# Attention and state-space layer on one core: first sample's remainders on VectorE, first row of maxima in halves, late inputs moved, the chain into the scan reordered

## The chip, the cores and the metric

The kernel runs on one core of one Trainium2 chip. What counts is its time on the device in microseconds (us). Time before: 542.61 us, median of 3 runs (541.83 to 543.48).

## What is computed

Eight samples of 256 tokens and 256 channels pass two layers, each with a residual. The reference, cut:

```python
# layer 1: modulated attention, 16 heads of 16 channels
x = x * s1; x = (x - mean) * rsqrt(var + 1e-5)
q, k, v = (x @ q_w.T) * q_dc, (x @ k_w.T) * k_dc, (x @ v_w.T) * v_dc * s2
out = softmax(q k^T / 4) v
x = x0 + (out @ w_w.T) * w_dc + (v @ u_w.T) * u_dc
# layer 2: a gated scan over the tokens, 512 channels, 16 states
xr, gate = split(x @ W_in.T); xc = silu(causal_conv4(xr + t_emb) + b_conv)
xn = layer_norm(xc) * ln_g + ln_b
Bm, Cm, dt = split(xn @ W_xproj.T)
Ad = 1 - 0.01 * tanh(dt @ W_dt.T + b_dt) * tanh(A_log)
Bd = Bm * minimum(norm(xn), 1)
def step(h, (ad, bd, xt, ct)):           # 256 steps
    h = clip(h * ad + bd * xt, -10, 10)
    return h, ct . h
return x + ((ys + D * xn) * silu(gate)) @ W_out.T
```

## The kernel before

Each engine has an instruction stream written out by hand, and semaphores order the streams against each other. An engine never takes a later instruction first: whatever stands behind a wait in its stream waits too. SP (and a little ScalarE) issue the DMAs, and SP too is one stream.

**Start.** VectorE multiplies the token tiles by the style (`modulated_statistics`, L1541), takes statistics (L1509, L1512), and makes the roots (`rsqrt`, L1518 to L1526); `demodulate` and a second `rsqrt` make the coefficients `dc`. TensorE transposes and projects (`channels_of`, L1023). q and k of a sample are split in three bf16 parts: ScalarE takes them from PSUM and casts (`take_qk`, L658, L662; `second_cast`, L667), GpSimd takes the two remainders of each (L501, L505, for all samples). The parts are stored to `qk_d` (`store_stack`, L295) and loaded again as a stack of rows per head (`load_stack`, L323), sample 0's in two halves, stacks 0 and 1 before, then x transposed, the in-weights, the norm rows and the out-weights (L364, L367), then stack 2.

**Attention.** For each sample TensorE makes every head's scores twice: once for the maxima (`max_scores`, L1049, reduced by VectorE, L1643), and once for the exponentials (`scores`, L1064; ScalarE, L737), for which the maxima of all heads stand as one more row of the stack. They get there by two transposes (`turn_maxima`, L1089), a copy to `mT` (L720) and a DMA (`take_maxima`, L722). While scores of sample b are made, the maxima of b+1 are. The stream for the first sample:

```python
            max_scores(0, 0, 8)
            pe.wait_ge(s["const_pool"], 1)
            pe.wait_ge(s["wgain"], 1)
            weight_sums()
            max_scores(0, 8, 12)
            pe.wait_ge(s["k_in"], 2)
            transpose_xn(2, 2)
            max_scores(0, 12, 14)
            pe.wait_ge(s["xnT_ready"], 3)
            channels_of(0, 2, "q_done")
            max_scores(0, 14, NH)
```

**Passage.** After the convolution the tiles are normalised on VectorE (`finish`: L1718, L1726). A tile `j` is split into three bf16 parts, `xpart`: the first by ScalarE (`leave_parts`, L851), the remainder by TensorE in PSUM (`first_left`, L1349), the second by ScalarE (`second_part`, L866), then `second_left` (L1356) and the third by VectorE (`last_part`, L1802). B is scaled by the norms (`square`, L859) and split (`split`, L1793 to L1797), stored and loaded across partitions (`store_b`, L273; `load_b`, L281), as are the tiles (`store_parts`, L388; `load_x`, L399). The gates are eight projections (`project_gate`, L1257) that end with `take_gate` (L820).

**Scan.** A step is a product on TensorE (`u_steps`, L1427) and one saturating operation on VectorE (L1834) in a ring of eight tiles `zst`, four of which lie in the in-weights `win`; every four steps TensorE reads the ring out (`y_steps`, L1438). The steps come in tiles of 16, with loads of x and B two tiles ahead on SP.

## Time and profile before

| | us |
|---|---|
| median of 3 runs | 542.61 |
| profiled execution | 539.56 |
| its span, first to last instruction | 537.8 |
| busy in it: TensorE, VectorE, ScalarE, GpSimd | 475.2, 432.0, 256.8, 177.5 |

The profiled execution is one run; its time holds the span and 1.8 us around it. A row of the timeline gives the start, the duration from first to last of its instructions, engine, line, operation and, in brackets, how long the engine sat idle before it and what released it. "q" behind an engine's name is its sequencer, which issues DMAs.

### The profile page before, as it was taken

The numbers are of one execution on the slowest core, as the hardware profiler recorded it, in microseconds if no ns is written. First come the engines' busy times: TensorE is split into PE (matmuls) and PEld (weight loads), VectorE is DVE, ScalarE is ACT, GpSimd is POOL, SyncE is SP. The second block draws the span as 40 slices with busy tenths as digits, with TensorE's granted clock in tenths as the row PEclk, the third lists the DMA queues.
The fourth block names the chain that finished last, engine by engine and source line by source line (L and its number), as shares of the span: only waits on it lengthen the run. The fifth ranks groups of instructions, "written<-read, shape, count | busy, mean of one in ns | idle before, by whom it ended". The sixth has DMA issues, their size and how long they took to land.

```text
span 537.8 us, 8609 instructions
## 1 busy us (share of the span) xinstructions
PE 475.2 (88%) x3062; PEld 286.3 (53%) x3082; DVE 432.0 (80%) x754; ACT 256.8 (48%) x512; POOL 177.5 (33%) x197
## 2 busy tenths in 40 slices
PE   6977699899999899888999888789999999999996
PEld 6744466768677566567887553233333333333333
DVE  6966257686766777749997977989999999999994
ACT  3442578757677546777777667343311111111111
POOL 5744303303023000000730002698783334333332
PEclk8879799999999999999999998999999999999999
DMA  8158864563545710110066377675546333333310
GB/s 313 39 177 212 318 175 90 153 173 92 138 109 135 177 40 2 41 40 1 2 247 195 110 247 175 223 239 195 165 138 157 117 117 112 107 104 105 105 37 22
DMA packets 45607, 71.81 MB, mean 134 GB/s; under 512 B 19098, under 2 KB 34074, under 8 KB 42893
## 3 DMA queue, kind: packets, MB, share of 16 engines
q1 hardware_dynamic: 37924, 65.64, 41.4%
q0 software_dynamic: 528, 3.55, 1.7%
q10 hardware_dynamic: 7112, 2.08, 1.6%
q8 instruction: 24, 0.39, 0.3%
q14 instruction: 19, 0.15, 0.1%
HBM read 41.88 MB, written 23.02 MB: 121 GB/s over the span
## 4 chain that ended last, share of the span: by engine, by line
PE 51%; DVE 31%; DMA 6%; ACT 6%; issue 3%; POOL 1%; ACTq 1%; SPq 0%; DVEq 0%
DVE win L1834 11%; PE bank L1023 6%; PE bank L1467 6%; PE bank L1079 5%; PE bank L1427 5%; PE bank L1438 5%; PE bank L1049 5%; PE bank L1064 5%; DVE z L1834 4%; PE bank L1128 3%; PE bank L1106 3%; DVE acc L1621 3%; DVE mx L1643 2%; PE bank L1097 2%; DVE zlast L1834 2%
## 5 line engine op out<-in xcount | busy, mean ns | idle before, releaser
L1643 DVE TENSOR_REDUCE mx<-bank 128x2 f32<-128x512 f32 x128 | 81.7, 686 | 61.0 <-PE bank L1049 60.9
L1427 PE MATMUL bank<-xst,bst 128*128 128x512 bf16 x238 | 76.3, 387 | 21.6 <-DVE win L1834 10.5
L737 ACT ACTIVATE ex<-bank 128x512 f32<-128x512 f32 x128 | 70.9, 599 | 40.8 <-PE bank L1064 40.8
L1834 DVE CUSTOM_DVE_ANT_0 win<-win,bank,hi 128x512 f32<-128x512 f32 x96 | 71.8, 748 | 3.4
L1427 PEld LDWEIGHTS bank<-xst,bst 128*128 128x128 bf16 x256 | 24.6, 97 | 70.7 <-DVE win L1834 31.9
L501 POOL TENSOR_TENSOR qk<-qk,part 128x512 f32<-128x512 f32 x16 | 21.9, 1372 | 108.9 <-ACT part L662 108.9
L1023 PE MATMUL bank<-xnT,w 128*128 128x256 f32 x192 | 51.1, 421 | 3.7 <-ACT xnT L647 1.8
L1064 PE MATMUL bank<-qst,kst 128*128 128x256 bf16 x256 | 46.8, 277 | 7.6 <-DMA qst<-mT 5.9
L1049 PE MATMUL bank<-kst,qst 127*128 127x256 bf16 x256 | 47.2, 277 | 6.3 <-DVE mx L1643 6.0
L605 POOL TENSOR_TENSOR yg<-yT,gateT 128x128 f32<-128x128 f32 x60 | 29.2, 519 | 57.3 <-ACT yT L956 57.3
L1023 PEld LDWEIGHTS bank<-xnT,w 128*128 128x128 f32 x192 | 39.5, 213 | 10.9 <-ACT xnT L647 2.5
L948 ACT ACTIVATE ytk<-bank,ybias 128x512 f32<-128x512 f32 x15 | 10.3, 687 | 68.5 <-PE bank L1438 68.5
L1079 PE MATMUL bank<-ex,vp 128*32 128x256 f32 x512 | 34.3, 385 | 5.6 <-ACT ex L737 5.6
L1621 DVE SCALAR_TENSOR_TENSOR acc<-xrp,wcv,acc 128x256 f32<-128x256 f32 x96 | 38.6, 478 | 0.6 <-ACT acc L702 0.6
L1467 PE MATMUL bank<-wo,yg 128*128 128x256 f32 x128 | 35.8, 403 | 0.2 <-DVE yg L1845 0.2
L1467 PEld LDWEIGHTS bank<-wo,yg 128*128 128x128 f32 x128 | 21.8, 189 | 26.4 <-issue 24.3
L1064 PEld LDWEIGHTS bank<-qst,kst 128*128 128x128 bf16 x256 | 23.0, 98 | 23.4 <-ACT ex L737 7.7
L1438 PE MATMUL bank<-win,cst 128*32 128x512 f32 x256 | 35.0, 619 | 0.0
L1438 PE MATMUL bank<-z,cst 128*32 128x512 f32 x128 | 33.7, 605 | 0.0
L1438 PE MATMUL bank<-lnb_rep,cst 128*32 128x512 f32 x64 | 33.5, 605 | 0.2 <-DVE zlast L1834 0.2
L1438 PE MATMUL bank<-zlast,cst 128*32 128x512 f32 x64 | 33.5, 605 | 0.0
L1049 PEld LDWEIGHTS bank<-kst,qst 127*128 127x128 bf16 x256 | 22.6, 99 | 18.8 <-DVE mx L1643 15.3
(209 smaller groups left out, 917.7 us busy)
## 6 DMA issues: line engine op xcount, KB each, us to landing
qk_d<-part SPq DMA_DIRECT2D x60, 96.0 KB, 2.4
xs_d<-xpart SPq DMA_DIRECT2D x15, 384.0 KB, 4.7
xst<-xs_d SPq DMA_DIRECT2D x15, 384.0 KB
xn_d<-xc SPq DMA_DIRECT2D x16, 256.0 KB, 3.9
xtk<-xn_d SPq DMA_DIRECT2D x64, 64.0 KB
xst<-xs_d SPq DMA_DIRECT2D x15, 256.0 KB
bd_d<-zeros POOLq DMA_DIRECT2D x1, 3468.0 KB, 13.0
qst<-qk_d SPq DMA_DIRECT2D x7, 384.0 KB, 4.0
```

Source lines behind the costliest of these rows:

```text
L605: ins = nc.gpsimd.tensor_tensor(yg[:, c, :].rearrange("p (b g k) -> p b g k", b=B, g=RG), yT[:, c, :].rearrange("p (k g b) -> p b g k", k= ...
L737: nc.scalar.activation(ex[:, n // 4, n % 4, :], bank[6 + n % 2][:, :], ACT.Exp, scale=SCALE)\
L1023: ins = mm(bank[bk][:, o * S:(o + 1) * S], w5[:, w, k, o * P:(o + 1) * P], xnT[:, k, :], start=k == 0, stop=k == HT - 1)
L1049: ins = mm(bank[4 + n % 2][:, t * S:(t + 1) * S], qstacks[b % NBUF][0:M_ROW, STACKED[n], t * P:(t + 1) * P], kstacks[b % NBUF][0:M_ROW, ST ...
L1064: ins = mm(bank[6 + n % 2][:, t * S:(t + 1) * S], kstacks[b % NBUF][:, STACKED[n], t * P:(t + 1) * P], qstacks[b % NBUF][:, STACKED[n], :] ...
L1079: ins = mm(bank[par][32 * r:32 * r + 32, o * S:(o + 1) * S], vp[:, b % 2, t, o * (NH // HT) + 4 * par + r, :], ex[:, g, r, t * S:(t + 1) * ...
L1427: mm(bank[t % 4][:, :], bst[:, slot, t % RS, :], xst[slot][:, t % RS, :], start=True, stop=True)\
L1438: ins = mm(bank[4 + i % 2][32 * k:32 * k + 32, :], cst[:, i % 2, 32 * (4 * g + k):32 * (4 * g + k) + 32], zst[(4 * g + k) % ZR], start=g = ...
L1467: ins = mm(bank[7][:, 0:H], yg[:, c, :], wo[:, c, :], start=False, stop=c == CT - 1, skip_group_check=True)
L1621: ins = v.scalar_tensor_tensor(acc[:, b % 2, c, :], xrp[:, b % 2, c, k:k + S], wcv[:, c, k:k + 1], acc[:, b % 2, c, :], ALU.mult, ALU.add)
L1643: v.tensor_reduce(mx[:, :, STACKED[n]:STACKED[n] + 1], bank[4 + n % 2][:, :].rearrange("p (t k) -> p t k", t=HALVES), AX.X, ALU.max)\
L1834: v._custom_dve(bass.dve_ops.TENSOR_ADD_SAT, out=zst[t % ZR], in0=zst[(t - 1) % ZR], in1=bank[t % 4][:, :], s0=hi[:, t:t + 1], s1=0.0).the ...
```

## The change

- VectorE makes sample 0's four remainders; GpSimd starts with sample 1, and fills the value tile when they are done. VectorE's products for samples 2 to 7 (`modulate`, a part of `modulated_statistics`) stand around them in three groups, their statistics and roots after the coefficients. ScalarE's root for them stands behind sample 1's casts.
- x transposed is loaded behind the first inputs; in-weights, norm rows, scan rates and out-weights after stack 2 has landed.
- The first eight heads' maxima of sample 0 are turned and moved to their row ahead (`turn_first_half`, `take_first_half`); scores of heads 0 and 1 of sample 0 stand ahead of maxima 15 and 16; scores 8 on wait for the second half.
- First parts of the first eight tiles are made by VectorE (`first_part`), third parts by ScalarE (`third_part`); the order on TensorE and ScalarE changes with them, and SP's order of the first stores and loads; one of the two first loads of B is SP's.
- The last gate's second half is projected among the scan's first steps. The ring begins in other tiles, so that the gate's part of `win` is first written in step 5, which waits for it.

```diff
@@ -200,8 +200,8 @@
-zst = [win[:, j // 2, (j % 2) * C:(j % 2 + 1) * C] for j in range(4)]
-zst += [lnb_rep[:, :, :].rearrange("p c q -> p (c q)"), z56[:, 0, :], z56[:, 1, :], zlast[:, :]]
+zst = [lnb_rep[:, :, :].rearrange("p c q -> p (c q)"), z56[:, 0, :], z56[:, 1, :]]
+zst += [win[:, k, half * C:(half + 1) * C] for half in range(2) for k in range(HT)] + [zlast[:, :]]
@@ -274,9 +274,9 @@
-def load_b(eng, i, name, lo=0, hi=RS):
-    for at, row, count in ((0, 0, 27), (33, 27, 24)):
+def load_b(eng, i, name, lo=0, hi=RS, groups=(0, 1)):
+    for at, row, count in [((0, 0, 27), (33, 27, 24))[j] for j in groups]:
@@ -314,6 +314,8 @@
+    sp.dma_start(xres[:, :, :], xT).then_inc(s["ld_x"], 16)
@@ -361,11 +363,12 @@
-    sp.dma_start(xres[:, :, :], xT).then_inc(s["ld_x"], 16)
+    stack(2)
+    sp.wait_ge(s["ld_q2"], 48)
+    sp.wait_ge(s["ld_k2"], 48)
...
-    stack(2)
@@ -430,18 +433,19 @@
-    store_xn(B - 1)
+    store_parts(B - 1, 0, FIRST, "xs_first")
...
-    store_parts(B - 1, 0, FIRST, "xs_first")
-    store_parts(B - 1, FIRST, RS, "xs_second")
...
+    sp.wait_ge(s["bd_first"], 16 * 7)
+    load_b(sp, 0, "ld_bf", 0, FIRST, (1,))
+    store_parts(B - 1, FIRST, RS, "xs_second")
+    store_xn(B - 1)
+    load_b(sp, 0, "ld_b0", FIRST)
...
-    sp.wait_ge(s["bd_first"], 16 * 7)
-    load_b(sp, 0, "ld_b0", FIRST)
@@ -483,12 +487,12 @@
-    pool.wait_ge(s["dc_done"], 1)
+    pool.wait_ge(s["part_ready"], 2)
...
-    for b in range(B):
+    for b in range(1, B):
@@ -714,12 +718,22 @@
+    def take_first_half():
+        act.wait_ge(s["mt_half"], 1)
+        nc.scalar.activation(mT[0:NH // 2, :], bank[3][0:NH // 2, 0:S], ACT.Copy).then_inc(s["mT_half"], 1)
+        act.wait_ge(s["mT_half"], 1)
+        act.dma_start(qstacks[0][M_ROW:P, 0:NH // 2], mT[0:NH // 2, :]).then_inc(s["m_half"], 16)
...
+        if b == 0:
+            act.wait_ge(s["m_half"], 16)
...
-        act.dma_start(qstacks[b % NBUF][M_ROW:P], mT[:, :]).then_inc(s["m_row"], 16)
+        lo = NH // 2 if b == 0 else 0
+        act.dma_start(qstacks[b % NBUF][M_ROW:P, lo:], mT[lo:, :]).then_inc(s["m_row"], 16)
@@ -742,13 +756,13 @@
+        if b == 0:
+            exponentials(0, 0, 2)
...
-            if b == 0:
-                exponentials(0, 0, 2)
@@ -795,8 +809,6 @@
-    nc.scalar.activation(rt[:, 2 * HALVES:], var_e[:, 2 * HALVES:], ACT.Sqrt).then_inc(s["rt_out"], 1)
-    act.wait_ge(s["rt_in"], 5)
@@ -806,8 +818,11 @@
+    act.wait_ge(s["rt_in"], 5)
+    nc.scalar.activation(rt[:, 2 * HALVES:], var_e[:, 2 * HALVES:], ACT.Sqrt).then_inc(s["rt_out"], 1)
...
+    take_first_half()
@@ -821,6 +836,13 @@
+    def take_half_gate(b, c2):
+        act.wait_ge(s["gate_done"], b * 2 + c2 + 1)
+        nc.scalar.activation(gateT[:, 2 * c2:2 * c2 + 2, b * S:(b + 1) * S],
+                             bank[gate_bank(b) + c2][:, :].rearrange("p (k s) -> p k s", k=2),
+                             ACT.Silu).then_inc(s["gate_out" if c2 else "half_gate"], 1)
@@ -854,10 +876,18 @@
+        if j < B:
+            act.wait_ge(s["xn_ready"], j + 1)
...
+    def third_part(j):
+        act.wait_ge(s["left_ready"], j + 1)
+        nc.scalar.activation(xpart[:, j % XRING, 2, :], bank[6 + j % 2][:, :], ACT.Copy)\
+            .then_inc(s["parts_ready"], 1)
@@ -893,45 +923,50 @@
-    leave_parts(0)
...
-    leave_parts(1)
...
-    leave_parts(2)
     second_part(1)
+    third_part(0)
     square(2)
-    leave_parts(3)
+    third_part(1)
     square(3)
+    second_part(2)
+    second_part(3)
+    third_part(2)
+    third_part(3)
...
-    second_part(2)
...
-    for j in range(4, B):
-        leave_parts(j)
-        second_part(j - 1)
-        if j in (5, 6):
+    square(4)
+    second_part(4)
+    for j in range(5, B):
+        square(j)
+        if j == B - 1:
+            act.wait_ge(s["sq_done"], B)
+            nc.scalar.activation(nrm[:, 0, :], ss[:, 0, :], ACT.Sqrt).then_inc(s["nrm_ready"], 1)
+        third_part(j - 1)
+        second_part(j)
+        if j < B - 1:
             split_d(j - 4)
-        square(j)
-    act.wait_ge(s["sq_done"], B)
-    nc.scalar.activation(nrm[:, 0, :], ss[:, 0, :], ACT.Sqrt).then_inc(s["nrm_ready"], 1)
+    third_part(B - 1)
     nc.scalar.activation(warm[:, :], ones[:, 0:1], ACT.Silu)
-    second_part(B - 1)
-    take_gate(4)
...
+    take_gate(4)
     act.wait_ge(s["bd_first"], 16 * 7)
-    load_b(act, 0, "ld_bf", 0, FIRST)
+    load_b(act, 0, "ld_bf", 0, FIRST, (0,))
...
-    take_gate(7)
+    take_half_gate(7, 0)
+    take_half_gate(7, 1)
@@ -1053,7 +1088,9 @@
-        if lo == 0:
+        if b == 0 and lo == 0:
+            pe.wait_ge(s["m_half"], 16)
+        if lo == (NH // 2 if b == 0 else 0):
@@ -1085,9 +1122,19 @@
+        if b == 0:
+            pe.wait_ge(s["mT_half"], 1)
...
+    def turn_first_half():
+        pe.wait_ge(s["vt_in"], 2)
+        pe.wait_ge(s["maxes"], NH // 2)
+        for t in range(HALVES):
+            ins = nc.tensor.transpose(bank[3][0:NH // 2, t * P:(t + 1) * P], mx[:, t, 0:NH // 2], ident[:, :])
+        ins.then_inc(s["mt_half"], 1)
@@ -1160,7 +1207,8 @@
-        scores(b, 0, 2)
+        if b >= 1:
+            scores(b, 0, 2)
@@ -1286,17 +1334,20 @@
-    pe.wait_ge(s["rt_in"], 5)
+    pe.wait_ge(s["rt_in"], 4)
...
+    max_scores(0, 8, 10)
+    turn_first_half()
     weight_sums()
-    max_scores(0, 8, 12)
+    max_scores(0, 10, 12)
...
+    scores(0, 0, 2)
@@ -1372,13 +1423,17 @@
-    project_gate(4)
+    first_left(2)
+    first_left(3)
+    second_left(2)
+    project_gate(4, 0, 2)
+    second_left(3)
+    project_gate(4, 2, 4)
...
-    first_left(2)
@@ -1388,25 +1443,22 @@
-    second_left(2)
     left_of_d(0)
-    first_left(3)
-    project_gate(5, 0, 1)
-    second_left(3)
...
-    project_gate(5, 1, 2)
+    project_gate(5, 0, 1)
...
+    project_gate(5, 1, 2)
...
-    project_gate(7)
+    project_gate(7, 0, 2)
@@ -1474,9 +1526,14 @@
+            if G == 0:
+                project_gate(7, 2, 3)
...
+                project_gate(7, 3, 4)
+                pe.wait_ge(s["half_gate"], 1)
+            if G == RG:
@@ -1567,17 +1628,28 @@
+    dve.wait_ge(s["cast0"], 1)
+    v.tensor_tensor(qk[:, 0, :], qk[:, 0, :], part[:, 0, 0, :], ALU.subtract).then_inc(s["rem_qk"], 1)
     dve.wait_ge(s["ld_rest"], 32)
-    modulated_statistics(2 * HALVES, NT)
+    modulate(2 * HALVES, 3 * HALVES)
+    dve.wait_ge(s["cast0"], 2)
+    v.tensor_tensor(qk[:, 1, :], qk[:, 1, :], part[:, 1, 2, :], ALU.subtract).then_inc(s["rem_qk"], 1)
+    for w in range(2):
+        dve.wait_ge(s["cast1"], w + 1)
+        v.tensor_tensor(part[:, w, 2 - 2 * w, :], qk[:, w, :], part[:, w, 1, :], ALU.subtract)\
+            .then_inc(s["part_ready"], 1)
...
-    dve.wait_ge(s["rt_in"], 5)
-    dve.wait_ge(s["rt_out"], 5)
+    modulate(3 * HALVES, 5 * HALVES)
+    dve.wait_ge(s["rt_in"], 4)
+    dve.wait_ge(s["rt_out"], 4)
...
-    roots(2 * HALVES, NT, 4)
+    modulate(5 * HALVES, NT)
+    statistics(xt, 2 * HALVES, NT)
+    roots(2 * HALVES, NT, 5)
@@ -1725,6 +1797,14 @@
+    def first_part(j):
+        b, t = FINISHED[j]
+        dve.wait_ge(s["xn_ready"], j + 1)
+        if j >= XRING:
+            dve.wait_ge(s[f"xs_out{j % XRING}"], 16 * (j // XRING))
+        v.tensor_copy(xpart[:, j % XRING, 0, :], xc[:, b * HALVES + t, :]).then_inc(s["part0"], 1)
@@ -1759,8 +1839,11 @@
-    finish((1,))
+    later = centre(1)
+    first_part(0)
+    scale(1, later)
     own.mark(v.tensor_tensor(raw[:, :, 0:2 * NS], raw[:, :, 0:2 * NS], wide.broadcast_to([P, NT, 2 * NS]), ALU.mult))
+    first_part(1)
@@ -1772,6 +1855,8 @@
+    first_part(2)
+    first_part(3)
@@ -1796,22 +1881,9 @@
-    def last_part(j):
-        dve.wait_ge(s["left_ready"], j + 1)
-        v.tensor_copy(xpart[:, j % XRING, 2, :], bank[6 + j % 2][:, :]).then_inc(s["parts_ready"], 1)
-    last_part(0)
-    finish((4,))
-    last_part(1)
-    finish((5,))
-    last_part(2)
-    finish((6,))
-    last_part(3)
-    finish((7,))
-    last_part(4)
-    last_part(5)
-    last_part(6)
+    for j in range(4, B):
+        finish((j,))
+        first_part(j)
@@ -1822,13 +1894,14 @@
-    last_part(7)
...
+        if t == 5:
+            dve.wait_ge(s["gate_done"], B * 2)
```

On TensorE, from the last projection of sample 1 into sample 0's attention (`L1049` and `L1084` are the scores for maxima, `L1064` and `L1101` those for exponentials, `mx` the maxima). Before:

```order
L1023 MATMUL bank<-xnT,w 128x256 x4
L1049 MATMUL bank<-kst,qst 128x256 x16
L1114 MATMUL bank<-wxg,ones 128x48 x4
L1114 MATMUL bank<-wx,lnb_rep 128x48 x4
L1049 MATMUL bank<-kst,qst 128x256 x8
L1015 MATMUL bank<-ident,xnb 128x128 x4
L1049 MATMUL bank<-kst,qst 128x256 x4
L1023 MATMUL bank<-xnT,w 128x256 x4
L1049 MATMUL bank<-kst,qst 128x256 x4
L1089 MATMUL bank<-ident,mx 16x128 x2
L1023 MATMUL bank<-xnT,w 128x256 x4
L1064 MATMUL bank<-qst,kst 128x256 x4
```

Now:

```order
L1084 MATMUL bank<-kst,qst 128x256 x20
L1136 MATMUL bank<-ident,mx 8x128 x2
L1161 MATMUL bank<-wxg,ones 128x48 x4
L1161 MATMUL bank<-wx,lnb_rep 128x48 x4
L1084 MATMUL bank<-kst,qst 128x256 x4
L1050 MATMUL bank<-ident,xnb 128x128 x4
L1084 MATMUL bank<-kst,qst 128x256 x4
L1058 MATMUL bank<-xnT,w 128x256 x4
L1101 MATMUL bank<-qst,kst 128x256 x4
L1084 MATMUL bank<-kst,qst 128x256 x4
L1128 MATMUL bank<-ident,mx 16x128 x2
L1058 MATMUL bank<-xnT,w 128x256 x4
```

The half turn (8 rows) comes after ten heads, and the first scores for exponentials stand ahead of the full turn instead of behind it.

On VectorE in the start, behind sample 1's normalisation, now:

```order
L1591 TENSOR_SCALAR xnb<-xt,mv,rs 128x256 x2
L1632 TENSOR_TENSOR qk<-qk,part 128x512
L1598 TENSOR_TENSOR xt<-xt,s1b 128x256 x2
L1636 TENSOR_TENSOR qk<-qk,part 128x512
L1639 TENSOR_TENSOR part<-qk,part 128x512 x2
L1607 TENSOR_SCALAR dcv<-bank 128x48
L1598 TENSOR_TENSOR xt<-xt,s1b 128x256 x4
L1575 RECIPROCAL dc<-dct 128x48
```

Four remainders have come in, and the twelve products, which stood together, are parted; six of them, the statistics and the roots follow the coefficients.

On SP, from the split of B to the store of the first tile's rest, now:

```order
L273 DMA bd_d<-bpart 16x8x16 x3
L402 DMA xst<-xs_d 24x4096
L402 DMA xst<-xs_d 16x4096
L402 DMA xst<-xs_d 8x4096
L281 DMA bst<-bd_d 24x1024
L391 DMA xs_d<-xpart 8x3x512
L385 DMA xn_d<-xc 128x512
L281 DMA bst<-bd_d 27x1024
L281 DMA bst<-bd_d 24x1024
L402 DMA xst<-xs_d 24x4096
L402 DMA xst<-xs_d 16x4096
L402 DMA xst<-xs_d 8x4096
L391 DMA xs_d<-xpart 112x3x512
```

A load of B (24x1024) and the store of a token tile have come in; both small stores of parts stood behind the first row before, now one stands ahead of it.

## Rows read from the trace of the kernel before

**Rows 1.** The page: its chain by engine, and its slices of DMA.

```profile
PE 51%; DVE 31%; DMA 6%; ACT 6%; issue 3%; POOL 1%; ACTq 1%; SPq 0%; DVEq 0%
...
DMA  8158864563545710110066377675546333333310
```

**Rows 2.** Timeline of TensorE, start: us, us, engine line op out<-in xcount [idle before <-releaser].

```profile
50.09 0.38 PE L1089 MATMUL bank<-ident,mx 128*16 128x128 f32 x2 [1.26 <-DVE mx L1643]
...
57.97 1.03 PE L1064 MATMUL bank<-qst,kst 128*128 128x256 bf16 x4 [5.04 <-DMA qst<-mT]
...
59.65 3.62 PE L1023 MATMUL bank<-xnT,w 128*128 128x256 f32 x8
```

**Rows 3.** DMA issues from 0 to 60 us: size, median us from issue to landing.

```profile
xres<-xT SPq DMA_DIRECT2D x1, 2048.0 KB, 11.2
...
win<-winT SPq DMA_DIRECT2D x1, 1024.0 KB, 13.1
```

**Rows 4.** The tile `mT`, its eight transfers.

```profile
DMA to landing us min/median/max: 1.8/1.8/7.0
```

**Rows 5.** Timeline of VectorE, scan steps 1 and 33.

```profile
326.81 0.75 DVE L1834 CUSTOM_DVE_ANT_0 win<-zlast,bank,hi 128x512 f32<-128x512 f32 x1 [2.79 <-PE bank L1427]
...
353.26 0.75 DVE L1834 CUSTOM_DVE_ANT_0 win<-zlast,bank,hi 128x512 f32<-128x512 f32 x1 [1.16 <-PE bank L1427]
```

**Rows 6.** Timeline of SP's issues, scan's beginning.

```profile
326.95 0.51 SPq L388 DMA_DIRECT2D xs_d<-xpart  x1
...
343.17 1.97 SPq L399 DMA_DIRECT2D xst<-xs_d  x3
```

**Rows 7.** Timeline of GpSimd, start.

```profile
15.18 1.80 POOL L487 MEMSET vp<- 128x2048 f32 x1 [7.38 <-DVE tick L1567]
...
18.37 5.75 POOL L501 TENSOR_TENSOR qk<-qk,part 128x512 f32<-128x512 f32 x2 [1.13 <-ACT part L662]
...
33.09 1.15 POOL L501 TENSOR_TENSOR qk<-qk,part 128x512 f32<-128x512 f32 x1 [6.75 <-ACT part L662]
```

**Rows 8.** Timeline of VectorE, start.

```profile
15.50 0.16 DVE L1522 TENSOR_TENSOR rt<-rt,var_e 128x2 f32<-128x2 f32 x1
15.70 1.31 DVE L1524 TENSOR_SCALAR rt<-rt 128x2 f32<-128x2 f32 x1
...
17.89 4.10 DVE L1541 TENSOR_TENSOR xt<-xt,s1b 128x256 f32<-128x256 f32 x12
...
33.14 1.19 DVE L1687 TENSOR_SCALAR lnb_rep<-ones,lnt 128x128 f32<-128x128 f32 x1
...
37.44 4.88 DVE L1643 TENSOR_REDUCE mx<-bank 128x2 f32<-128x512 f32 x8 [2.46 <-PE bank L1049]
```

**Rows 9.** Timelines of SP and ScalarE, start: first stack, exponentials of heads 2 and 3.

```profile
26.37 1.96 SPq L295 DMA_DIRECT2D qk_d<-part  x4
31.32 1.87 SPq L323 DMA_DIRECT2D qst<-qk_d  x3
...
63.73 1.24 ACT L737 ACTIVATE ex<-bank 128x512 f32<-128x512 f32 x2 [0.75 <-PE bank L1064]
```

**Rows 10.** Windows: us, busy PE, PEld, DVE, ACT, POOL, PEclk, DMA share, GB/s.

```profile
58.00:59.00 1.00, 1.00 (x5) 0.68 (x6) 0.00 (x0) 0.39 (x1) 0.00 (x0) 0.50 0.98 410
...
330.00:332.00 2.00, 2.00 (x9) 0.26 (x9) 1.93 (x3) 2.00 (x4) 0.00 (x0) 0.55 0.27 22
```

**Rows 11.** Passage: VectorE's timeline, ScalarE's issues, the chain (start us, us, what).

```profile
295.28 0.29 DVE L1767 COPY cdt<-raw 128x256 f32<-128x256 f32 x1
...
318.21 1.30 ACTq L273 DMA_DIRECT2D bd_d<-bpart  x3
...
322.31 3.73 DMA bst<-bd_d
```

**Rows 12.** Timelines of ScalarE's issues and TensorE, sample 1's row.

```profile
77.30 0.54 ACTq L722 DMA_DIRECT2D qst<-mT  x1
...
80.16 0.60 PE L1064 MATMUL bank<-qst,kst 128*128 128x256 bf16 x4
```

6 lines of the change are left out of this document (4 added, 2 removed).

## The prediction, on record before the run

> **What bounds the kernel now.** I read the page's chain first [rows 1]: TensorE is on it for 51% of the span and VectorE for 31%, so the bound changes by stage. Its busy slices give the stages: attention to about 235 us is TensorE's, the scan from 327 us VectorE's. Neither one's steady part is edited. What is left is the start (to 64 us) and the passage into the scan (290 to 353 us). These two I read in the timeline, engine by engine, with the DMA issues beside them.
>
> Start: the scores of sample 0 begin at 57.97, after 5.04 us in which TensorE waits for the row of maxima to land in the stack [rows 2]. Behind SP's queue lay x transposed (2 MB), the in-weights and more [rows 3]; the row took 7.0 us to land, where the median of its eight is 1.8 [rows 4].
>
> Passage: the first scan step on VectorE is at 326.81, a step takes about 0.78, and the 33rd waits 1.16 us for TensorE at 353.26 [rows 5]. TensorE had to wait there for the load issued by SP at 343.17. That was the 18th of SP's issues in an unbroken row, which began when the store issued at 326.95 had landed [rows 6]. **So up to step 32 the scan is bound by SP's queue, not by its own start.** A scan that starts earlier wins only what SP wins.
>
> **The change, part by part.** The sum is made against the profiled execution: span 537.8, its time 539.56; the median of the runs, 542.61, is 3.05 higher, and the difference is taken over to it.
>
> *Sample 0's remainders on VectorE.* On GpSimd the first two took 5.75 us together, although one alone takes 1.15 [rows 7]: VectorE's twelve products ran meanwhile, 17.89 to 21.99 [rows 8]. Now the four are VectorE's, each of twice a product's width (0.34), so 0.68. From 18.37, when GpSimd could begin: remainder to 19.05; two products; the second cast is done at 19.95, remainder to 20.7; ScalarE's second casts (0.63 each) end at 20.57 and 21.41; the last remainders end at 22.15. Before, SP's stores waited for them until 26.37: 4.2 us earlier. SP issued the first loads at 31.32 [rows 9], now at 27.1, all six by 30.9.
>
> But VectorE pays. It still has: demodulation 0.2, four products 1.4, a wait for ScalarE's root (which stands behind its 2.0 us of store issues, 22.2 to 24.5), the coefficients 1.8 (end 26.3, before 30.6), six products 2.05, statistics of twelve tiles 4.0+0.9 and the variances (end 33.55), roots 1.35 with ScalarE's share, projection weights 1.75, one normalisation 0.7: 37.4. GpSimd's last remainder for sample 1 (32.95 to 34.1) can hold up a single-input operation of VectorE, as at 33.14, where one took 1.19 [rows 8] beside GpSimd's at 33.09 [rows 7]: its like before take 0.28, so up to +0.9; I take +0.6. The first maximum is at **38.0, against 37.44** [rows 8]. The half stack is there long before (30.9+2.5), TensorE is free at 31.1; both now wait for VectorE. This part brings the stacks 4 us and costs the path 0.6.
>
> In those four products' time GpSimd fills the value tile (1.80, [rows 7]). While it did so before, an operation of VectorE took 1.31 at 15.70 instead of 0.17. By that row alone the products could be held 1.8 us, and the sum would be 1.8 less. I take 0: the two-input operation at 15.50, in the same fill, took its usual 0.16 [rows 8]. The Trainium skill ("SBUF — State Buffer", Who interferes with whom) says a VectorE instruction with two SBUF inputs contends with a GpSimd instruction that reads SBUF, not with one that only writes it; by that rule too the products aren't held, but remainders of sample 1 on GpSimd would be, as far as they meet VectorE's products. By my times they just don't (products end at 28.4, GpSimd starts at 28.6).
>
> *First row in halves.* Maxima 1 to 8 (4.88 us, [rows 8]) end at 42.9; the half turn (0.38, as [rows 2]) and ScalarE's copy 0.4 follow; issue at 43.9. TensorE still has weight sums 1.7, scores for maxima, transposes and a projection (1.73), and wants the half row at 38.0+11.1=49.1. In 1.8 to 4 us it lands by 48. Two scores (0.44) and the half turn lengthen this piece by about 0.65: the full turn ends at **51.7, against 50.47** [rows 2]: +1.2. From there nothing waits for a row until head 8, some 8 us on. The path is then ScalarE's: copy 0.4, q 0.85+0.6, k 0.85+0.6, GpSimd's remainder 1.15, cast 0.6, with gaps 6.0: exponentials of heads 2 and 3 at 57.7. TensorE needs less, 4.7; one of its two projections took 3.4 of the 3.62 at 59.65 [rows 2], since the granted clock had fallen to 0.50, that is 1.2 GHz, after the idle stretch [rows 10]; without that stretch I take 1.73. Before, these exponentials began at 63.73 [rows 9]. **Term A: -6.0 us.** It stays in the span: later samples are tied to one another and to nothing in the start.
>
> *Late inputs elsewhere.* x transposed is issued at about 9.0. DMA is busy a tenth in the slice from 13 to 27 us [rows 1], so it lands there; nobody waits for it. The other four (2.3 MB) are issued when stack 2 has landed, about 72: cost 0, they are wanted over 100 us later. Behind them on SP stand the moves of sample 0's output and stack 3, each with some us to spare.
>
> *Passage.* First parts become casts in SBUF on VectorE (eight), third parts go from VectorE to ScalarE. A copy of half the size took 0.29 [rows 11], so a first part costs 0.29 to 0.58; I take 0.4. Four now stand ahead of the reciprocal: +1.6 on its chain. TensorE's back transposes follow all of gate 4 and end at 306.6 instead of 303.7. From there ScalarE's row is two copies, the bias, four times square, third and second part (0.5 to 0.75 each) and two casts. I get VectorE's split done at 317.15 against 318.12. ScalarE then has the last third part (to 316.7) and a table load of 1.28 before its store: 318.1, against 318.21: nothing won. The B load is split over two queues, so one issue (1.0) goes: data at 325.0 instead of 326.04 [rows 11]. Scan start -1.1.
>
> SP: between the split and the store of the first tile's rest it has one B load and one token store more, one small store less (+0.9 us), about 0.3 us less of waits, and starts 0.95 earlier: 326.6 against 326.95 [rows 6]. **Term B: -0.4**, by SP, at the 33rd step; -1.1 if SP gains as the scan start does.
>
> *Half gate in the scan.* Two pieces (0.86 each) stand between the first steps. Step 5 waits for the second, which follows u 7, which needs z 4: 0.45 us late. SP's wait at step 32 swallows it. At the low clock seen at 330 to 332 [rows 10] a piece takes 1.73 and step 8 comes 2.9 late instead of 0.3; SP swallows about 2: term B +0.5.
>
> **Sum:** -6.0-0.4=-6.4: span 531.4, profiled execution 533.2, median 536.2. Its own range, with an error of 1 us in each term, is 534.8 to 538.2.
>
> **Rivals.**
> 1. *The late loads meet sample 1's row.* It is issued at 77.30-6.0=71.3, and stack 2 lands near 72. If it takes 7.0 instead of 1.8, TensorE, with 1.1 us to spare (77.30+1.8 against 80.16, [rows 12]), waits 4.1: -2.3, **540.3**. For: the same four loads stood before the 7.0. Against: they come a little after the row, and without x transposed. Chance 0.15. The Trainium skill ("DMA: Bandwidth & Descriptors", Queues, rings and completion order) has each DMA engine take turns between the issuers' queues packet by packet, so the row would not wait for SP's backlog; the 7.0 agrees only as far as it is under the 11.2 of x transposed [rows 3].
> 2. *VectorE as the new bound of the start.* The fill holds the products, or sample 1's remainders meet them: first maximum at 39.8, term A -4.2: **538.0**. Then remainders on VectorE don't do what they should. For: the 1.31 [rows 8]. Chance 0.15.
> 3. *The half row is late: slower.* TensorE is in order, and the wait for the half row stands ahead of the last two maxima, the turn and all of attention. It has 49.1-43.9=5.2 us; beyond, each us is lost, and everything at 5.2+6.4=11.6 us to landing. If the row is held like SP's loads (13.1 for the in-weights, [rows 3]), it costs 7.9: **544.1**. Only stack 1's loads are under way then, no megabytes behind them. Chance 0.04.
> 4. *SP lets go.* Term B -1.1, and GpSimd doesn't hold VectorE (-0.6): **534.9**. Chance 0.12.
>
> **Chances.** Forecast 0.52, rivals 0.15, 0.15, 0.04, 0.12; 0.02 for what I don't see. About 0.3% (1.6 us) can be told from no change. Faster: all but rival 3 and the far end of rival 1, 0.93; within 0.3%: 0.04; slower: 0.03. The range takes in rivals 2, 4 and most of 1: 534.0 to 540.8.
>
> **What would show it.** Right: sample 0's last remainders end near 22; first maximum near 38 though its stack landed by 34; no wait over 1 us for the row in samples 0 and 1; exponentials of heads 2 and 3 near 57.7; sample 1's row lands in about 2 us; scan start some 7 us earlier, while the 33rd step waits more than 1.16. Wrong: several us of wait for the half row or in sample 1; a first maximum beyond 39.5; step 5 more than 1 us late; a scan start later than 321.

## The result, and the profile after

The changed kernel takes **543.06 us** (median of 12 runs, 541.65 to 549.01), the kernel before, on the same chip, 541.57 (12 runs, 539.91 to 543.48): a ratio of 1.0044, 95% interval 1.0024 to 1.0064. Forecast was 536.2 and "faster". It is slower by 1.5 us by the medians; 0.44% would be 2.4 us, since the runs of the change spread further upward than those of before.

The profiled execution of after is a long one: 547.56 us, span 544.4. That of before was a short one (539.56, span 537.8). Their difference of 6.6 in the span is more than the 1.5 of the medians; one reason for such differences, the clock in the start, turns out to be one of the causes (below). The page of after, its chain by engine, granted clock and DMA in slices of 13.6 us; [rows 1] has the first and last of these of before:

```profile
PE 51%; DVE 28%; DMA 7%; ACT 5%; issue 4%; SPq 3%; POOL 1%; ACTq 0%; another core or an unknown queue 0%; DVEq 0%
...
PEclk8695999999999999999899998999999999999999
...
DMA  8666077753636450101038466686446434333310
```

SP's queue is on the chain with 3%, where it had nothing. Three places tell the story. The first is VectorE in the start, by the columns of [rows 8]:

```profile
21.26 0.69 DVE L1636 TENSOR_TENSOR qk<-qk,part 128x512 f32<-128x512 f32 x1 [1.32 <-ACT part L666]
21.87 1.47 DVE L1639 TENSOR_TENSOR part<-qk,part 128x512 bf16<-128x512 f32 x2
...
23.38 1.42 DVE L1598 TENSOR_TENSOR xt<-xt,s1b 128x256 f32<-128x256 f32 x4
28.45 0.45 DVE L1575 RECIPROCAL dc<-dct 128x48 f32<-128x48 f32 x1 [3.66 <-ACT dct L812]
...
37.23 0.77 DVE L1571 TENSOR_SCALAR var_e<-mv 128x12 f32<-128x12 f32 x1
...
41.74 4.87 DVE L1715 TENSOR_REDUCE mx<-bank 128x2 f32<-128x512 f32 x7
```

The remainders end at 23.3 (forecast 22.15, before 26.3). Then VectorE waits 3.66 us for ScalarE's root, and the first maximum starts at 41.74, not at 38.0. What ScalarE did:

```profile
26.26 0.60 ACT L651 ACTIVATE xnT<-bank 128x512 f32<-128x512 f32 x1 [3.64 <-PE bank L1058]
26.28 1.78 ACTq L295 DMA_DIRECT2D qk_d<-part  x4
28.11 0.24 ACT L812 ACTIVATE dct<-dcv 128x48 f32<-128x48 f32 x1 [1.25 <-issue]
```

Ahead of the stores and the root in its stream stands `take_xn(1, 0)`, the copy of sample 1's transposed input, and it waits until TensorE has projected sample 0's v (L1058). TensorE, in the start and behind its wait for the maxima:

```profile
22.87 3.29 PE L1058 MATMUL bank<-xnT,w 128*128 128x256 f32 x8
...
35.02 0.60 PE L1084 MATMUL bank<-kst,qst 127*128 127x256 bf16 x4
42.49 1.21 PE L1084 MATMUL bank<-kst,qst 127*128 127x256 bf16 x4 [6.86 <-DVE mx L1715]
...
48.09 1.78 PE L1161 MATMUL bank<-wxg,ones 128*128 128x48 f32 x8
...
53.97 3.18 PE L1058 MATMUL bank<-xnT,w 128*128 128x256 f32 x8
56.99 0.60 PE L1101 MATMUL bank<-qst,kst 128*128 128x256 bf16 x4
...
59.24 0.38 PE L1128 MATMUL bank<-ident,mx 128*16 128x128 f32 x2 [1.21 <-issue]
```

It idles 6.86 us. Its granted clock falls from 1.00 to 0.50 (2.4 to 1.2 GHz) at about 39 us, in the idle stretch, and stays there until about 56:

```profile
36.00:44.00 8.00, 1.33 (x5) 0.39 (x6) 7.27 (x34) 1.55 (x5) 3.99 (x3) 0.71 0.46 100
44.00:52.00 8.00, 7.54 (x33) 4.86 (x33) 4.30 (x7) 0.37 (x1) 4.93 (x2) 0.50 0.79 197
```

The wait of 5.04 us for the row [rows 2] is indeed gone: the scores at 56.99 wait for nothing. But the full turn is at 59.24, where it was at 50.09.

The second place is sample 2. SP's issues there:

```profile
82.75 0.36 SPq L371 DMA_DIRECT2D win<-winT  x1
...
87.78 5.43 SPq L295 DMA_DIRECT2D qk_d<-part  x8
98.89 1.81 SPq L325 DMA_DIRECT2D qst<-qk_d  x3
100.74 1.86 SPq L325 DMA_DIRECT2D kst<-qk_d  x3
```

ScalarE's issue of the row, and TensorE's next scores:

```profile
100.83 0.54 ACTq L736 DMA_DIRECT2D qst<-mT  x1
```
```profile
106.19 0.61 PE L1101 MATMUL bank<-qst,kst 128*128 128x256 bf16 x4 [2.35 <-DMA qst<-mT]
```

Stack 3's loads are issued beside sample 2's row, not ahead of it, and the row lands 5.3 us after its issue (median before 1.8, [rows 4]). SP had waited 4.9 us for stack 2 to land ahead of the late inputs, and 5.6 us for stack 3's stores to land ahead of its loads. The third place, the scan's start on VectorE, answers to [rows 5]:

```profile
332.72 0.75 DVE L1907 CUSTOM_DVE_ANT_0 lnb_rep<-zlast,bank,hi 128x512 f32<-128x512 f32 x1 [2.83 <-PE bank L1479]
...
337.53 1.53 DVE L1907 CUSTOM_DVE_ANT_0 win<-win,bank,hi 128x512 f32<-128x512 f32 x2 [0.88 <-PE bank L1305]
...
346.80 0.75 DVE L1907 CUSTOM_DVE_ANT_0 lnb_rep<-zlast,bank,hi 128x512 f32<-128x512 f32 x1 [0.69 <-PE bank L1479]
```

The scan starts 5.9 later than before, attention's fourth row (below) came 7.3 later: the passage won 1.4. The scan gave 0.8 back: 0.88 for the half gate (`t == 5` in the code, the sixth step, which the prediction calls step 5), 0.69 at the 17th step and 0.63 further on, less 1.16 at the 33rd and 0.30 at the 9th that before waited and after does not.

The start of ScalarE's copy of the full row of maxima, one per sample, is a good mileage post. All kernels are told by it. From sample 3 on every kernel but one (i3_later) has 22.57 us between two posts until sample 6, to within 0.2, so what happened earlier is all in four numbers. The posts are of one profiled execution each. "Before" is its median beside the kernel, on the same chip; it moved between 540.82 and 541.57 from chip to chip, so a difference of about 1 us between kernels of different rows decides nothing unless their intervals stand apart.

| kernel | sample 0 | 1 | 2 | 3 | median us | before | ratio (95%) |
|---|---|---|---|---|---|---|---|
| before | 50.51 | 76.90 | 97.42 | 121.04 | | | |
| after | 59.66 | 78.64 | 100.42 | 128.32 | 543.06 | 541.57 | 1.0044 (1.0024 to 1.0064) |
| e1_rem | 58.85 | 81.94 | 105.00 | 127.57 | 545.18 | 541.05 | 1.0069 (1.0045 to 1.0093) |
| e2_half | 54.64 | 73.65 | 95.65 | 118.22 | 537.79 | 541.05 | 0.9931 (0.9910 to 0.9951) |
| e3_late | 53.27 | 75.83 | 96.35 | 124.09 | 542.61 | 541.05 | 1.0021 (1.0004 to 1.0037) |
| e4_pass | 55.01 | 78.89 | 101.46 | 124.04 | 540.51 | 541.05 | 0.9987 (0.9969 to 1.0004) |
| f1_root | 55.58 | 74.56 | 96.27 | 123.72 | 541.89 | 541.57 | 1.0007 (0.9988 to 1.0025) |
| f2_norem | 54.67 | 73.66 | 94.70 | 122.41 | 540.76 | 541.57 | 0.9990 (0.9971 to 1.0009) |
| f3_nolate | 58.98 | 77.97 | 101.05 | 123.61 | 540.47 | 541.57 | 0.9965 (0.9942 to 0.9988) |
| h1_halfpass | 55.01 | 74.00 | 95.90 | 118.48 | 536.59 | 541.57 | 0.9915 (0.9890 to 0.9941) |
| i2_rem | 55.80 | 74.79 | 96.82 | 119.39 | 537.75 | 540.82 | 0.9932 (0.9907 to 0.9958) |
| i3_later | 56.24 | 75.22 | 97.96 | 120.53 | 543.34 | 540.82 | 1.0025 (0.9996 to 1.0054) |
| j1_nohg | 53.84 | 72.83 | 97.85 | 120.42 | 536.71 | 540.82 | 0.9916 (0.9887 to 0.9945) |
| k1_fill | 52.49 | 71.47 | 98.40 | 120.97 | 538.23 | 540.82 | 0.9934 (0.9913 to 0.9955) |
| m1_fillx | 52.18 | 71.17 | 93.02 | 115.59 | 533.34 | 541.17 | 0.9854 (0.9831 to 0.9878) |
| m2_early | 55.57 | 74.56 | 96.67 | 119.24 | 536.05 | 541.17 | 0.9897 (0.9878 to 0.9915) |
| m3_fillearly | 51.98 | 70.96 | 92.72 | 115.29 | 532.58 | 541.17 | 0.9835 (0.9815 to 0.9854) |
| m4_afterfill | 54.85 | 74.93 | 96.74 | 123.84 | 539.24 | 541.17 | 0.9966 (0.9946 to 0.9985) |
| n1_mended | 53.73 | 72.72 | 94.69 | 117.26 | 535.13 | 540.90 | 0.9905 (0.9873 to 0.9938) |
| n2_nohg | 52.85 | 71.84 | 93.78 | 116.35 | 532.47 | 540.90 | 0.9846 (0.9816 to 0.9875) |

### The profile page after: what moved, and what is told of

It is laid out like the page before. It is cut to its first block, busy times and chain, and to the rows that moved or that the text cites. A ratio compares the mean times of both kernels' runs of the same rounds, so it can differ in the third digit from the quotient of the medians.

```text
span 544.4 us, 8627 instructions
## 1 busy us (share of the span) xinstructions
PE 480.1 (88%) x3064; PEld 291.9 (54%) x3084; DVE 431.6 (79%) x758; ACT 257.9 (47%) x513; POOL 170.7 (31%) x193
## 4 chain that ended last, share of the span: by engine, by line
PE 51%; DVE 28%; DMA 7%; ACT 5%; issue 4%; SPq 3%; POOL 1%; ACTq 0%; another core or an unknown queue 0%; DVEq 0%
DVE win L1907 9%; PE bank L1058 6%; PE bank L1519 5%; DVE z L1907 5%; PE bank L1479 5%; PE bank L1490 5%; PE bank L1084 4%; PE bank L1116 4%; PE bank L1175 4%; PE bank L1101 3%; PE bank L1144 3%; DVE lnb_rep L1907 3%; PE bank L1305 2%; PE bank L1376 2%; PE bank L1153 2%
## 5 line engine op out<-in xcount | busy, mean ns | idle before, releaser
L1490 PE MATMUL bank<-win,cst 128*32 128x512 f32 x256 | 67.3, 605 | 0.2 <-DVE zlast L1907 0.2
L1084 PE MATMUL bank<-kst,qst 127*128 127x256 bf16 x256 | 49.2, 288 | 12.3 <-DVE mx L1715 11.1
L1058 PE MATMUL bank<-xnT,w 128*128 128x256 f32 x192 | 51.3, 422 | 2.6 <-ACT vp L686 1.4
L1101 PE MATMUL bank<-qst,kst 128*128 128x256 bf16 x256 | 46.2, 273 | 6.3 <-DMA qst<-mT 3.2
L505 POOL TENSOR_TENSOR qk<-qk,part 128x512 f32<-128x512 f32 x14 | 16.2, 1156 | 110.8 <-ACT part L666 110.8
L1058 PEld LDWEIGHTS bank<-xnT,w 128*128 128x128 f32 x192 | 39.9, 216 | 10.0 <-ACT vp L686 1.7
L1084 PEld LDWEIGHTS bank<-kst,qst 127*128 127x128 bf16 x256 | 23.2, 101 | 25.4 <-DVE mx L1715 19.9
L1101 PEld LDWEIGHTS bank<-qst,kst 128*128 128x128 bf16 x256 | 22.5, 97 | 22.2 <-ACT ex L751 9.5
```

Source lines behind the costliest of these rows:

```text
L1058: ins = mm(bank[bk][:, o * S:(o + 1) * S], w5[:, w, k, o * P:(o + 1) * P], xnT[:, k, :], start=k == 0, stop=k == HT - 1)
L1084: ins = mm(bank[4 + n % 2][:, t * S:(t + 1) * S], qstacks[b % NBUF][0:M_ROW, STACKED[n], t * P:(t + 1) * P], kstacks[b % NBUF][0:M_ROW, ST ...
L1101: ins = mm(bank[6 + n % 2][:, t * S:(t + 1) * S], kstacks[b % NBUF][:, STACKED[n], t * P:(t + 1) * P], qstacks[b % NBUF][:, STACKED[n], :] ...
L1490: ins = mm(bank[4 + i % 2][32 * k:32 * k + 32, :], cst[:, i % 2, 32 * (4 * g + k):32 * (4 * g + k) + 32], zst[(4 * g + k) % ZR], start=g = ...
```

## The experiments

### Each part alone

Four kernels: before, with one part of the change each. e1_rem has sample 0's remainders on VectorE and the reordered chain:

```diff
-            for b in range(B):
+            for b in range(1, B):
...
+            dve.wait_ge(s["cast0"], 1)
+            v.tensor_tensor(qk[:, 0, :], qk[:, 0, :], part[:, 0, 0, :], ALU.subtract).then_inc(s["rem_qk"], 1)
...
+            modulate(5 * HALVES, NT)
+            statistics(xt, 2 * HALVES, NT)
+            roots(2 * HALVES, NT, 5)
```


> Sample 0's remainders on VectorE with the reordered chain behind them, and nothing else of the change. Theory A (ScalarE's queue): the root of the coefficients stands on ScalarE behind the copy of sample 1's transposed input, which waits for TensorE's value projection, and behind the stores; VectorE idles 3 to 4 us for it near 25 to 28 us, its statistics come behind that, the first maximum is near 41.7 (before 37.4), TensorE is idle for over 5 us ahead of its third score and its granted clock falls; part of this is swallowed, since the row still waits for x transposed: 543 to 546 against 541.6. Rival B (VectorE's work is harmless, the loss in the change comes from elsewhere): first maximum before 39, time within 541 to 542.

Measured: first maximum at 41.54, row copy of sample 0 at 58.85, 545.18: theory A's case. This part alone costs 4.1 us.

e2_half has the first row in halves:

```diff
+            max_scores(0, 8, 10)
+            turn_first_half()
             weight_sums()
-            max_scores(0, 8, 12)
+            max_scores(0, 10, 12)
...
+            take_first_half()
```


> Only the first row in halves, with the exponentials of heads 0 and 1 ahead of the row's second copy; remainders on GpSimd, late inputs where they were. Theory A: the half row is issued near 43.5, before x transposed (48.6), and lands in 2 to 3 us; the 5.0 us of wait of TensorE go, but the full row still meets x transposed and the in-weights and lands near 58, when heads 8 to 15 want it only near 60: 537 to 539. Rival B (halves cost the change its gain): the half turn and the two scores stand in a stretch of low clock and the second half of the row is waited for: 541 to 544.

Measured: 537.79, 3.3 us faster than before: theory A's case. Exponentials of heads 2 and 3 start at 60.91 (63.73 in [rows 9]).

e3_late moves the late inputs only:

```diff
+            sp.dma_start(xres[:, :, :], xT).then_inc(s["ld_x"], 16)
...
             stack(1)
-            sp.dma_start(xres[:, :, :], xT).then_inc(s["ld_x"], 16)
+            stack(2)
+            sp.wait_ge(s["ld_q2"], 48)
+            sp.wait_ge(s["ld_k2"], 48)
```


> Only x transposed ahead and the other late inputs behind stack 2. Theory A: the row lands in 1.8 us, the wait of 5.0 us goes, sample 1's offset is -4.5; but SP waits for stack 2's landing, so stack 3's loads are issued after sample 2's row instead of before it, the row takes over 4 us and TensorE loses 2 to 3.5 us of it: 538 to 540. Rival C: stack 3 is in time here, since stack 2 is earlier than in the change: 536.5 to 537.5. Rival D: x transposed in the start (13 to 22 us) holds the start's own loads or lowers the clock: over 541.

Measured: the mechanism is theory A's, the size was underrated. The wait for sample 0's row is gone, but from sample 2 to 3 it takes 27.7 us, 5.2 more than the steady 22.57, and the time is 542.61: the part costs 1.6 on balance. A time over 541 is what rival D named too. Its two signs speak otherwise: the first maximum is at 37.31 (before 37.44), so the start's own loads are not held, and the clock's fall (0.57 from 38 to 50 us) comes in e4_pass as well, where x transposed is not moved.

e4_pass has the passage and the half gate, and before's start:

> Only the passage and the half gate in the scan. Expected from the change's profile: scan start 1.4 us earlier than before, 0.9 us lost at step 5 and 0.7 at step 17, the 1.2 us at step 33 gone: 540.5 to 541.5, within 0.2% of before. Rival: the stalls come from the low clock at the start of the scan and vary, then up to 542.5.

Measured: 540.51, 0.5 less than before but within its interval. Its start is before's, instruction by instruction, and yet its row copy is at 55.01 against 50.51, while the first maximum is at 37.76 against 37.44. The projections on TensorE, of this run and of before, tell why:

```profile
49.75 3.15 PE L1044 MATMUL bank<-xnT,w 128*128 128x256 f32 x8
```
```profile
46.41 1.99 PE L1023 MATMUL bank<-xnT,w 128*128 128x256 f32 x8
```

**In the execution whose profile the prediction read, TensorE had the full clock from 37 to 57 us (after two stretches at 0.50 before that); in this one the clock was at 0.50 from about 38 to 52.** At sample 3's post the two are 3.0 us apart (124.04 and 121.04), which is what the median of before lies above its profiled execution (3.05). Against e4_pass the changed kernel's sample 1 is level (78.64 and 78.89), and all its loss stands between samples 2 and 3 (27.90 against 22.58).

The parts add up: 4.1 - 3.3 + 1.6 - 0.5 = 1.9, measured for the whole 1.5. That is partly luck: f2_norem and f3_nolate, below, have three parts each, and neither is what its parts add up to.

### The change with one part taken back or mended

f1_root is the whole change with ScalarE's root ahead:

```diff
-            take_xn(1, 0)
+            act.wait_ge(s["rt_in"], 4)
+            nc.scalar.activation(dct[:, 2:, :, :], dcv[:, 2:, :, :], ACT.Sqrt).then_inc(s["rt_out"], 1)
             act.wait_ge(s["part_ready"], 2)
             store_stack(act, 0, range(NH // HT // 2, NH // HT))
-            act.wait_ge(s["rt_in"], 4)
-            nc.scalar.activation(dct[:, 2:, :, :], dcv[:, 2:, :, :], ACT.Sqrt).then_inc(s["rt_out"], 1)
+            take_xn(1, 0)
```


> The whole change, but on ScalarE the root of the coefficients stands ahead of the copy of sample 1's transposed input and of the stores. Theory A (ScalarE's queue): VectorE's wait of 3.7 us at 28.4 goes, the first maximum is at 37.5 to 38.5 instead of 41.7, and the time is 538.5 to 540.5. Rival (VectorE's own work, remainders and statistics in that order, is the bound): the first maximum stays beyond 40.5 and the time at 542 or more. In both sample 2's row still lands late.

VectorE's timeline of f1_root:

```profile
24.14 0.44 DVE L1575 RECIPROCAL dc<-dct 128x48 f32<-128x48 f32 x1
...
38.24 5.46 DVE L1715 TENSOR_REDUCE mx<-bank 128x2 f32<-128x512 f32 x8
```

The wait of 3.66 is gone and the first maximum is where the prediction had it. But this profile differs from that of after by more than the edit: TensorE's projection of v took 1.89 us in it, not 3.29. A run shown below, i3_later, has the stream of the change up to here, unedited, and such a projection too. TensorE, then VectorE in i3_later:

```profile
21.92 1.89 PE L1057 MATMUL bank<-xnT,w 128*128 128x256 f32 x8
```
```profile
26.38 0.45 DVE L1574 RECIPROCAL dc<-dct 128x48 f32<-128x48 f32 x1 [2.25 <-ACT dct L811]
...
39.50 2.68 DVE L1714 TENSOR_REDUCE mx<-bank 128x2 f32<-128x512 f32 x4
```

So of the 3.5 us between 41.74 and 38.24 the queue's order made 1.3 (39.50 against 38.24), and the low clock under the projection and what stands ahead of it on TensorE, for which the order makes VectorE wait, the other 2.2. The time missed the expected range: 541.89, only 1.2 under the change and barely clear of the noise. TensorE still idles (4.53 us) and its clock still falls, and samples 2 to 3 still take 27.45. So the queue is a cause, but not the only one.

f2_norem leaves the remainders on GpSimd; f3_nolate leaves the late inputs in their old place. Their edits are those of e1_rem and e3_late, undone.

> The whole change without the remainders and the reordered chain (they stay on GpSimd, statistics ahead of the coefficients as before). If the parts add up: 541.1 + 1.6 (late inputs) - 3.3 (halves) - 0.5 (passage) = 538.9. If the late inputs' loss grows once the halves make the samples earlier (row of sample 2 still amid stack 3's loads, TensorE waiting over 3 us): 540 to 541.5. If stack 2 is early enough for stack 3 to be in time: 536 to 537.

Measured 540.76: the second case, 0.8 under before where its parts add up to 2.2 under. Samples 2 to 3 take 27.71.

> The whole change with the late inputs left where they were (x transposed and the in-weights behind stack 1). If the parts add up: 541.1 + 4.1 - 3.3 - 0.5 = 541.4. Sample 2's row is issued over 3 us behind the last load of stack 3, lands in 2 to 3 us, and the distance from sample 2's row to sample 3's is 22.6 to 23.6 us instead of 27.9. Rival: the distance stays at 27 or more; then the late inputs are not what holds that row.

Measured 540.47, 1.1 under before where its parts add up to 0.3 above; samples 2 to 3 take 22.56. The late inputs' place is what holds that row, and it is worth 2.6 us against the change.

> Only the two parts that measured a gain: halves of the first row, and passage with the half gate. Adding up: 541.1 - 3.3 - 0.5 = 537.3, faster than both kernels. Rival: they share a gain, 538 to 539.

Its edits are e2_half's and e4_pass's together. Measured **536.59**, 5.0 us faster than before, 6.5 faster than the change.

### What is wrong with the remainders and the late inputs

i2_rem is h1_halfpass with e1_rem's and f1_root's edits.

> Halves and passage, plus the remainders on VectorE with the root of the coefficients ahead on ScalarE; late inputs where they were before. If ScalarE's queue was all that was wrong with the remainders, this is faster than halves and passage without them (536.6): the stack is there 3 us earlier, 533.5 to 535.5. If VectorE's statistics, roots and weights stand ahead of the first maximum anyway (theory A's second half: first maximum near 38, as without the remainders), the remainders bring nothing: 536.5 to 538.

Measured 537.75, first maximum 38.42: the second case. Against h1_halfpass it is no faster (1.2 us slower by the medians, and their intervals overlap). The stack is there 3 us earlier and nobody uses it, since VectorE's statistics, roots and weights stand ahead of its first maximum.

i3_later moves the four late inputs once more:

```diff
             for b in range(1, B):
                 move_att(b - 1)
+                if b == 2:
+                    for dst, src in ((win[:, :, :], winT), (lnr[:, :, :], ln_row.partition_broadcast(P)),
+                                     (tA[:, :], alog_row.partition_broadcast(P)), (wo[:, :, :], woT)):
+                        sp.dma_start(dst, src).then_inc(s["ld_l2"], 16)
```


> The whole change, but SP no longer waits for stack 2, and the four late inputs are issued behind the second sample's output moves, when stack 3 is loaded. If it is their place ahead of stack 3 that costs (stores of stack 3 held up, its loads amid sample 2's row), the distance from sample 2's row to sample 3's falls from 27.9 to 22.6 to 23.6 us and the time is 539.5 to 541, near the kernel that left them in place (540.5). If 2.3 MB beside attention cost wherever they stand, the loss shows one sample later and the time stays at 542.5 to 544.

Measured 543.34: the second case. Samples 2 to 3 take 22.57, but samples 3 to 4 take 29.0. SP's issues of this run, around stack 3 and around stack 4:

```profile
85.09 3.90 SPq L295 DMA_DIRECT2D qk_d<-part  x8
90.97 2.28 SPq L325 DMA_DIRECT2D qst<-qk_d  x3
...
102.78 0.58 SPq L372 DMA_DIRECT2D win<-winT  x1
...
106.78 4.58 SPq L295 DMA_DIRECT2D qk_d<-part  x8
116.56 1.81 SPq L325 DMA_DIRECT2D qst<-qk_d  x3
```
and its chain there (start us, us, what):
```profile
120.93 6.30 DMA qst<-mT
```

From its first store to its first load a stack takes 5.9 us with nothing beside it, and 9.8 behind the late inputs: its stores take longer to land (5.8 us instead of 2.4), and SP waits for them ahead of the loads.

j1_nohg is h1_halfpass without the half gate:

```diff
-            project_gate(7, 0, 2)
+            project_gate(7)
...
-                    if G == 0:
-                        project_gate(7, 2, 3)
...
-                if t == 5:
-                    dve.wait_ge(s["gate_done"], B * 2)
```


> Halves and passage without the half gate among the scan's steps: gate 7 is complete ahead of the scan, VectorE waits for nothing at step 5. In the traces TensorE idles 2.2 us ahead of the scan for B when the half gate is moved, and VectorE then loses 0.7 to 1.0 us at step 5 and about as much at step 9 to 17. So this is 0.5 to 1.5 us faster than with the half gate (536.6): 535.1 to 536.1. Rival: gate 7 ahead of the scan holds the first products, the scan starts 1 us later and the two are equal.

Measured 536.71 against 536.59: no difference. The wait at `t == 5` (0.67 in e4_pass, 0.99 in h1_halfpass) goes, but one at the 17th step (0.97 in both h1_halfpass and this) stays; the half gate is neither gain nor loss. The two profiles show something else too. Their starts are the same code, this one's was 1.2 us ahead at sample 1's post, and at sample 2's it was 1.95 behind: its row of sample 1, issued 1.2 us earlier and so closer behind stack 2's loads, took 5.6 us to land instead of 4.2.

### The clock, and the backlog

k1_fill adds matmuls that nobody reads to h1_halfpass, into a PSUM bank not yet in use:

```diff
+            fill(36)
             v_tokens(0)
+            fill(20)
             pe.wait_ge(s["v_in"], 1)
             channels_of(2, 3, "vt_done")
             pe.wait_ge(s["rt_in"], 5)
-            max_scores(0, 0, 8)
+            fill(24)
+            for n in range(8):
+                max_scores(0, n, n + 1)
+                fill(2)
```


> Halves and passage, with 96 matmuls of 128 columns of ones into a bank that nobody reads, in TensorE's idle stretches between 28 and 42 us. They add work and order nothing else. If the low granted clock after the idle stretch is what makes the start long, the clock stays at 1.00 from 28 to 52 us, weight sums take 0.99 instead of 1.78 us and the projection at 49 takes 1.9 instead of 3.3; sample 0's full row comes 2 to 4 us earlier and the time is 533 to 535. If the fillers only delay (or the clock falls all the same), it is 536.6 to 538.

Windows of k1_fill, then of h1_halfpass, columns as in [rows 10]:

```profile
36.00:44.00 8.00, 5.27 (x53) 3.48 (x50) 5.01 (x9) 1.56 (x4) 7.79 (x5) 1.00 0.68 173
44.00:52.00 8.00, 6.53 (x48) 5.24 (x48) 4.93 (x10) 3.34 (x5) 1.59 (x1) 1.00 0.75 183
```
```profile
36.00:44.00 8.00, 6.32 (x29) 2.99 (x28) 6.17 (x10) 1.97 (x5) 7.79 (x4) 0.71 0.78 196
44.00:52.00 8.00, 8.00 (x33) 6.74 (x33) 2.58 (x4) 1.88 (x2) 1.29 (x1) 0.51 0.80 201
```

The clock holds, and sample 0's row copy comes 2.5 us earlier. The time does not: 538.23 against 536.59, where their intervals overlap, so that it is no faster and perhaps slower. In the profile all is lost, and more, at sample 1 (26.9 us to the next post, 21.9 in h1_halfpass), whose row is now issued at 71.88, beside stack 2's loads (68.87 to 72.5):

```profile
71.88 7.59 DMA qst<-mT
```

(the chain of k1_fill: start us, us, what). SP's issues of stack 2, first store and first load:

```profile
60.41 4.62 SPq L295 DMA_DIRECT2D qk_d<-part  x8
68.87 1.77 SPq L323 DMA_DIRECT2D qst<-qk_d  x3
```

The DMA queues of k1_fill from 71.9 to 76.0 us: q1 is SP's, and the row's own queue, q10, is not among them. Its first packet starts after 76.

```profile
q1 hardware_dynamic: 161, 0.90, 102.7%
```

Stack 2's stores, at 60.41, stand behind x transposed and the in-weights: 8.5 us from first store to first load. m1_fillx takes x transposed out of the way, as the change does; m2_early and m3_fillearly move all five late inputs there, without and with fillers (the edit of m2_early against h1_halfpass):

```diff
+            sp.dma_start(xres[:, :, :], xT).then_inc(s["ld_x"], 16)
+
+            for dst, src in ((win[:, :, :], winT), (lnr[:, :, :], ln_row.partition_broadcast(P)),
+                             (tA[:, :], alog_row.partition_broadcast(P)), (wo[:, :, :], woT)):
+                sp.dma_start(dst, src).then_inc(s["ld_l2"], 16)
...
             stack(1)
-            sp.dma_start(xres[:, :, :], xT).then_inc(s["ld_x"], 16)
...
```


> The kernel with fillers (halves, passage, fillers), and x transposed issued at 9 us; the other four late inputs stay behind stack 1. If the 2 MB of x transposed are what delays stack 2's stores and loads (60.4 to 72.5 there), stack 2's loads are issued 2 us earlier, sample 1's row no longer waits 4.6 us, and the 2.5 us of the clock come through: 534 to 535.5. If sample 1 loses over 3 us all the same, stack 2 is bound by its own chain of parts, stores and loads: 537.5 to 538.5.

> Halves and passage, with all five late inputs issued at 9 to 12 us, when DMA was idle from 15 to 26. No backlog then stands beside any stack of samples 1 to 3. If a late input costs only by standing beside a stack, nothing is lost: 535.5 to 536.6, the distances between the rows of samples 1, 2 and 3 all 21 to 23 us. If the transfers reach into sample 0's stores at 26 us and hold them, the first maximum is over 38.5 and the time over 537.5.

> Both: fillers on TensorE, and all five late inputs at 9 to 12 us. If clock and backlog are the two causes and independent, sample 0's row is 2.5 us earlier than without fillers, none of it is lost at samples 1 to 3, and the time is 533 to 534.5. If the stacks' own chain is the bound of samples 1 and 2 (SP's stores, loads and landing), the gain of the fillers is lost there again: 536 to 538.

Measured 533.34, 536.05 and **532.58**. Stack 2 in m3_fillearly, SP's issues and the chain:

```profile
59.90 3.66 SPq L295 DMA_DIRECT2D qk_d<-part  x8
65.51 1.77 SPq L328 DMA_DIRECT2D qst<-qk_d  x3
```
```profile
71.36 4.03 DMA qst<-mT
```

5.6 us from store to load, a row that lands in 4.0, and the fillers' gain comes through and more: 532.58 against 536.05 without them, where the post of sample 3 is 3.95 earlier. Neither alone can be told from h1_halfpass (k1_fill +1.6, m2_early -0.5, with intervals that overlap its own); together they bring 4.0. m1_fillx and m3_fillearly can't be told apart either: moving x transposed is enough, as far as these runs can tell.

m4_afterfill puts fillers into the changed kernel, 112 of them in the idle stretch behind `max_scores(0, 0, 2)`:

> The whole change with 148 fillers on TensorE between 31 and 46 us, 112 of them in the idle stretch of 6.9 us ahead of its third score. They cannot move the first maximum (41.7, set by VectorE). If the clock made the other half of the start's loss, weight sums take 0.99 instead of 1.78 us, the projection behind them 1.9 instead of 3.2, and sample 0's last maximum ends near 55.5 instead of 59.1; the time then falls by up to 3.5, unless stack 2 or 3 is late and takes it: 540 to 543. If the clock is no cause, the last maximum stays at 58 or later.

TensorE's timeline of m4_afterfill:

```profile
34.86 6.42 PE L1314 MATMUL bank<-warm_up 128*128 128x128 bf16 x112
...
46.53 0.99 PE L1161 MATMUL bank<-wxg,ones 128*128 128x48 f32 x8
...
50.24 1.89 PE L1058 MATMUL bank<-xnT,w 128*128 128x256 f32 x8
```

First maximum 41.15, nearly as in the change, but the row copy at 54.85 instead of 59.66, and 539.24 instead of 543.06, below the expected range. The clock cost the change 4.8 us of its start in the profile and 3.8 in the median. Samples 2 to 3 still take 27.1.

n1_mended is the whole change with f1_root's edit, fillers (128 of them; the expectation's 132 is a miscount) and all late inputs early; n2_nohg is m3_fillearly without the half gate.

> All five parts of the change, with the root of the coefficients ahead on ScalarE, 132 fillers on TensorE, and all five late inputs at 9 to 12 us. Against the same kernel without the remainders on VectorE (532.6): if the remainders are worth the 3 us that the first stack comes earlier, 529.5 to 531. If VectorE's statistics, roots and weights stand ahead of the first maximum all the same (38.2), it is 532 to 534. If the late inputs now stand beside sample 0's stores, which come at 23 instead of 26 us, the first stack loses its lead and it is 533 or more.

> Halves, passage, fillers, all five late inputs early, but gate 7 complete ahead of the scan. Against 532.6 with the half gate: with it VectorE lost 0.55 us at step 5 in the profile; without it TensorE has 1.7 us more ahead of the scan's first product, of which 2.2 us were idle. Expected 532 to 533, the same within what can be told; if gate 7 holds the first product, 533.5.

Measured 535.13 and 532.47. n1_mended is its expectation's third case: the remainders now cost 2.5 us (against m3_fillearly). Sample 0's stores are issued at 22.6, into the late inputs (the DMA engines are busy all the time from 12 to 27 us), and ScalarE waits for its own to land before it may overwrite `qk`; VectorE waits for ScalarE, so that the first maximum is at 40.15. Timelines of n1_mended, ScalarE's, then VectorE's:

```profile
30.31 0.84 ACT L660 ACTIVATE qk<-bank,dc 128x256 f32<-128x256 f32 x2 [3.74 <-DMA qk_d<-part]
```
```profile
35.80 0.23 DVE L1584 RECIPROCAL rs<-rt 128x12 f32<-128x12 f32 x1 [2.73 <-ACT rt L820]
```

So m3_fillearly and n2_nohg are about 8.5 us faster than before and over 10 faster than the change, with fillers and without the remainders on VectorE. How much of the 8.5 the kernel before would gain from fillers and early inputs alone, without the halves, no run shows. Not tried either: the roots and weights of VectorE behind its first maxima, by which the earlier stack might be of use.

## Why the prediction was wrong

**The step that failed first: "a wait for ScalarE's root (which stands behind its 2.0 us of store issues, 22.2 to 24.5)".** It stands behind the stores *and* behind `take_xn(1, 0)`, which waits for TensorE's projection of v, done near 26.2. The reading was of the stores' place in the stream, not of the whole stream. VectorE waited 3.66 us there, and the first maximum came 3.7 us late (41.74 for 38.0). With that projection at full clock the same stream waits 2.25 and has its first maximum at 39.50 (i3_later); with the root ahead it is at 38.24. So the step is worth 1.3 us at full clock, and the rest of the 3.7 is the clock's doing, through that wait.

**The second: "without that stretch I take 1.73" for a projection.** The forecast took TensorE's clock as full once the wait for the row was gone. The change makes another idle stretch, of 6.86 us, ahead of the third score, and the clock fell there. The prediction had what would have warned it: its own times left TensorE free at 31.1 and the first maximum at 38.0, and it had seen a projection of 3.4 us at 0.50 [rows 2, 10]. With fillers in the idle stretch the time was 3.8 us lower (m4_afterfill), the most that any single mending of the change won. And it laid its sum on a profile that had the full clock from 37 to 57 us and took the 3.05 us to the median over as a constant; e4_pass shows that the start is where such executions differ.

**The third: late inputs, "cost 0 ... stack 3, each with some us to spare".** Stack 3 had nothing to spare. Before, its last load was issued at 96.3 and sample 2's row at 97.8, and TensorE already waited for that row, a line of the trace of before that the prediction did not read:

```profile
101.71 0.61 PE L1064 MATMUL bank<-qst,kst 128*128 128x256 bf16 x4 [0.88 <-DMA qst<-mT]
```

Moved behind stack 2, the 2.3 MB and SP's wait for that stack's landing put stack 3's loads at 98.9, and sample 2 lost 5.3 us in the profile, 2.6 in the median (f3_nolate). Rival 1 had the mechanism, one sample early: by its row, sample 1 would lose.

**Right:** the half row lands in time and the 5.04 us of wait go (e2_half, -3.3). It is smaller than the 6.0 of term A by the clock: the exponentials of heads 2 and 3, forecast for 57.7, begin at 60.91 in e2_half and at 58.22 in m3_fillearly, where the clock holds (in after at 65.91, before at 63.73). Right too that VectorE's own work keeps the first maximum at 38 however early the stack is (38.24 in f1_root, 38.42 in i2_rem; the +0.6 for GpSimd was there, as 0.96 at another operation); from that alone the remainders had nothing to give, and all of term A belonged to the halves. Term B was -0.4; scan start -1.4 (forecast -1.1), the scan's end -0.6 and e4_pass's median -0.5. The half gate costs 0.9 at its wait instead of 0.45, and leaving it out wins nothing (j1_nohg): swallowed, as forecast.

That term B fits is in part luck. The forecast let SP's queue hold the 33rd step, which was to wait more than 1.16. In after it does not wait at all: it starts at 359.33, so that of attention's 7.3 us of delay 1.2 are made good there, which is rival 4's case (-1.1). The 0.6 that then go again are a wait for TensorE at 422.6, which the prediction doesn't have. The range was looser than its working: an error of 1 us in each of two terms gives 534.2 to 538.2 if they add, not 534.8 to 538.2; the measured time is outside every version.

Of the rivals, 2 had the sign that came (first maximum beyond 39.5), but not its cause and not its price (538.0). Rival 3's 544.1 is near the measured time by luck: no wait of TensorE for the half row is in the profile. The fill did not hold the products. Four of them took 1.42 us from 23.38 on while GpSimd filled `vp` (23.40 to 25.20). By the Trainium skill ("SBUF — State Buffer", Who interferes with whom), too, a GpSimd instruction that only writes does not hold them: the trace agrees.

## What to carry to other kernels

A sum over one engine's work is only as good as the list of everything that stands ahead of each wait: for an instruction that is to come earlier, write out the whole stream ahead of it on its own engine. Where transfers are moved, ask of every stack or row behind them how much it has to spare now, from the rows (issue, landing, who waited), before a cost of 0 is written; an earlier start is worth only what the next transfer lets through. And a gain that rests on a short stretch at full clock needs the idle stretch ahead of it mended too, and more than one profile of the start: two profiles of one stream can differ by the clock as much as by an edit.

## What the runs showed of the hardware

Matmuls into an unused bank can keep the clock, though not in every profile. In after it fell to 0.50 in the idle stretch of 6.86 us; with 112 matmuls of 128 columns in that stretch (6.42 us busy) it was 1.00 from 28 to 52 us, and weight sums took 0.99 instead of 1.78. It was 1.00 there in k1_fill, m3_fillearly and n1_mended too; m1_fillx had 0.52 from 28 to 30 us, and n2_nohg, with the same 96 fillers, 0.66 from 40 to 45.

A row of 8 KB on ScalarE's queue took 7.59 us (k1_fill) while SP's queue had stack 2's loads (1.5 MB) to move; with the last load issued 2.2 us ahead of it, it took 4.03 (m3_fillearly), and 1.8 with none. In k1_fill the wait was ahead of its first packet: between 71.9 and 76.0 us 161 packets of SP's queue started, 0.90 MB, which kept the 16 engines full, and none of the row's. By the Trainium skill ("DMA: Bandwidth & Descriptors", Queues, rings and completion order) each DMA engine takes turns between queues packet by packet, so that a short transfer would not have to wait out another queue's whole backlog; but such a packet is a bundle, typically of 9 to 17 descriptors, that is drained before the engine turns. The 161, some ten per engine, do not contradict that if each of them is one descriptor. Whether the row waited in the engines or its issue was processed late, no run here shows.
